# Feed-forward weights rounded and split by pieces of three tiles instead of tile by tile

## The reference

```
x = x + gate_msa * (attention(modulate(layernorm(x))) @ W_proj + b_proj)
x = x + gate_mlp * (gelu(modulate(layernorm(x)) @ w1 + b1) @ w2 + b2)
```

## Time and profile before

| | |
|---|---|
| median of 3 runs | 2257.18 us (2246.01 to 2261.7) |
| profiled execution | span 2257.0 us; no time around the span is listed for it |
| mean granted clock of TensorE | 0.932 of full speed |
| PE busy | 2033.0 us, 90% of the span |
| DVE busy | 1335.6 us, 59% |
| ACT busy | 1143.6 us, 51% |
| DMA | 173.97 MB moved, mean 77 GB/s |
| instructions | 38969 |

### The profile page before, as it was taken

One profiled execution on the slowest core, in us unless ns is written; L12 is line 12 of the kernel. 1 busy time (PEld: TensorE's weight loads), 2 busy tenths in 40 slices (PEclk: granted clock), 3 DMA queues, 4 the chain that ended last, 5 costly groups with the idle time before them and its releaser, 6 DMA issues.

```text
span 2257.0 us, 38969 instructions
## 1 busy us (share of the span) xinstructions
PE 2033.0 (90%) x15592; PEld 1509.0 (67%) x15592; DVE 1335.6 (59%) x2940; ACT 1143.6 (51%) x1705; POOL 207.4 (9%) x311
## 2 busy tenths in 40 slices
PE   6978899899989998999799899899888898999898
PEld 4347388658966994788375657788786556464658
DVE  4757637756774767476556673462444849484833
ACT  2444624574655456445626464552443464637373
POOL 2000001202100211012010000011000000000001
PEclk9787989899989999999889999998898998999999
DMA  5333332343333233333322313346254141314011
GB/s 158 77 123 57 100 95 72 79 111 86 89 77 106 72 89 76 96 94 88 94 72 35 103 17 65 73 88 109 34 95 130 7 121 26 99 11 115 9 14 25
DMA packets 204731, 173.97 MB, mean 77 GB/s; under 512 B 54822, under 2 KB 164678, under 8 KB 204550
## 3 DMA queue, kind: packets, MB, share of 16 engines
q1 hardware_dynamic: 197974, 158.76, 30.1%
q0 software_dynamic: 6576, 12.71, 2.1%
HBM read 125.57 MB, written 40.11 MB: 73 GB/s over the span
## 4 chain that ended last, share of the span: by engine, by line
PE 63%; DVE 18%; ACT 12%; DMA 3%; issue 2%; SPq 2%; POOL 0%; ACTq 0%; POOLq 0%; DVEq 0%
PE PSA L1856 16%; PE PSA L1871 13%; DVE MX L1496 7%; PE PSA L1647 5%; PE PSA L1760 5%; PE PSA L1737 5%; ACT PB L1345 4%; PE PSA L1707 4%; PE PSA L1750 4%; PE PSA L1719 2%; DVE FL L1396 2%; PE PSA L1780 1%; ACT FH L1375 1%; PE PSA L1670 1%; DVE HH L1626 1%
## 5 line engine op out<-in xcount | busy, mean ns | idle before, releaser
L1496 DVE TENSOR_REDUCE MX<-PSA 128x1 f32<-128x512 f32 x768 | 490.4, 682 | 296.9 <-PE PSA L1737 293.2
L1856 PE MATMUL PSA<-A,FH 128*128 128x256 f32 x2520 | 445.3, 292 | 12.5 <-DVE HH L1626 9.6
L1871 PE MATMUL PSA<-FH,HH 128*128 128x288 f32 x2016 | 447.7, 313 | 2.0 <-DVE HH L1626 2.0
L1382 ACT ACTIVATE HH<-PSA 128x512 fp32r<-128x512 f32 x252 | 150.4, 597 | 572.5 <-PE PSA L1856 567.3
L1345 ACT ACTIVATE PB<-PSA 128x1024 f32<-128x1024 f32 x384 | 370.9, 1025 | 102.5 <-PE PSA L1750 101.8
L1856 PEld LDWEIGHTS PSA<-A,FH 128*128 128x128 f32 x2520 | 364.9, 195 | 34.6 <-issue 17.3
L1871 PEld LDWEIGHTS PSA<-FH,HH 128*128 128x128 f32 x2016 | 329.7, 195 | 42.3 <-issue 38.0
L1871 PE MATMUL PSA<-FL,HH 128*128 128x288 f32 x1008 | 303.7, 301 | 0.0
L1737 PE MATMUL PSA<-KS,QS 54*128 54x512 f32 x768 | 226.1, 517 | 40.0 <-DVE MX L1496 14.0
L1255 POOL TENSOR_TENSOR X<-X,TM 128x288 f32<-128x288 f32 x128 | 101.1, 808 | 1496.7 <-DVE TM L1561 1496.6
L1760 PE MATMUL PSA<-PB,VT 128*32 128x512 f32 x1536 | 219.6, 637 | 0.0
(11 more groups left out here) (166 smaller groups left out, 2261.5 us busy)
## 6 DMA issues: line engine op xcount, KB each, us to landing
qkd<-HH SPq DMA_DIRECT2D x48, 504.0 KB
ST<-in_L_cond_w SPq DMA_DIRECT2D x51, 432.0 KB
ST<-in_L_cond_w SPq DMA_DIRECT2D x102, 192.0 KB
QS<-qkd SPq DMA_DIRECT2D x88, 144.0 KB
KS<-qkd SPq DMA_DIRECT2D x88, 144.0 KB
QS<-qkd SPq DMA_DIRECT2D x144, 72.0 KB
KS<-qkd SPq DMA_DIRECT2D x144, 72.0 KB
ST<-in_L_cond_w SPq DMA_DIRECT2D x153, 48.0 KB
```

Source lines behind the costliest of these rows:

```text
L1382: e.activation(r(HH[u][:, 0, :]), PS[bk][:, :], gelu)
L1496: e.reduce_max(MX[p // 2 % 2][:, col:col + 1], PS[bk][:, :], axis=AX.X).then_inc(free[bk], 1)
L1856: m = e.matmul(PS[bk][:, s_ * 256:(s_ + 1) * 256], r(w_), r(x_[:, half * 256:(half + 1) * 256]), start=(z == 0), stop=(z == 6))
L1871: m = e.matmul(PS[bk][:, 0:C], r(HH[u][:, c, tk]), r(w_), start=False, stop=(j == NCH - 1 and z == 2))
```

## The change

The three instructions per tile become three per piece. `prep_f` is called once per piece, when the `fc2` of slot 2, 5 or 8 has been put. One cast on ACT takes 128 x 2016 elements and waits for the last uses of all three slots. One subtraction on DVE corrects the tail rows of the three tiles (33 x 3 x 128, a pattern with a stride from tile to tile), one writes the low parts of the three (128 x 3 x 544). All three tiles of a piece count as ready when these are done (`w_ready` is the same count for all). The transfers, the buffers, the matmuls and every other weight stay.

```diff
@@ plan(), prep_f
-    n_f, f_at, b2_free = [0], [0], {}
+    n_f, b2_free = [0], {}
 
     def prep_f():
-        n_ = n_f[0]
-        k, x = n_ // 3, n_ % 3
+        k = n_f[0]
         if k >= len(PIECES):
             return
         n_f[0] += 1
+        n_ = 3 * k
         if n_ % NCH == 0:
             put("b2in", k, n_ // NCH)
-        if x == 0:
-            yield from arrive(("f", k))
-            f_at[0] = stage(("f", k))
-        at, m = f_at[0], n_split[0]
+        yield from arrive(("f", k))
+        at, m = stage(("f", k)), n_split[0]
         n_split[0] += 1
-        put("split", ("f", n_), at, landed[at], m, w_free.get(("F", n_ % NCH)))
+        put("split", ("f", n_), at, landed[at], m, [w_free[("F", n_ % NCH + x)] for x in range(3) if ("F", n_ % NCH + x) in w_free])
         yield
         yield
         yield
         put("fix", ("f", n_), at, m)
-        w_ready["f", n_] = m + 1
+        for x in range(3):
+            w_ready["f", n_ + x] = m + 1
+        left[at] = ("split", m + 1)
         yield
-        if x == 2:
-            left[at] = ("split", m + 1)
-            ahead()
-            yield
+        ahead()
+        yield
         if n_ % NCH == 0:
             put("b2", n_ // NCH, b2_free.get(n_ // NCH % 2))
             yield
@@ ffn_steps, fc2
-                    bg.append(prep_f())
+                    if j % 3 == 2:
+                        bg.append(prep_f())
@@ before the loop over the items
-    bg += [prep_f() for _ in range(NCH)]
+    bg += [prep_f() for _ in range(NCH // 3)]
@@ split_of
-            return (FH[:, j * NHT:(j + 1) * NHT], FL[:, j * NLT:(j + 1) * NLT], key[1] % 3 * NHT, NHT, NLT,
-                    (NLT, 128))
+            return (FH[:, j * NHT:(j + 3) * NHT], FL[:, j * NLT:(j + 3) * NLT], 0, 3 * NHT, NLT, (NLT, 128))
@@ act_program, split
-                    if old is not None and key[0] == "f":
-                        w.wait_ge(*old)
+                    if key[0] == "f":
+                        for done in old:
+                            w.wait_ge(*done)
@@ dve_program, fix
+                    if key[0] == "f":
+                        def three(t, p0, p1, f0, step, n):
+                            return view(t, p0, f0, [(1, p1 - p0, True), (step, 3, False), (1, n, False)])
+
+                        st = ST[k % 2][:, :]
+                        e.tensor_tensor(r(three(hi, 64, R2 - 1, f0, NHT, nf)), three(st, 64, R2 - 1, f0, NHT, nf),
+                                        three(hi, 64, R2 - 1, f0, NHT, nf), ALU.subtract).then_inc(s_wfix, 1)
+                        e.tensor_tensor(r(three(lo, 0, 128, 0, NLT, nl)), three(st, 0, 128, 0, NHT, nl),
+                                        three(hi, 0, 128, 0, NHT, nl), ALU.subtract).then_inc(s_wlo, 1)
+                        continue
```

## The result

The changed kernel takes 2341.35 us (median of 4 runs, 2336.54 to 2343.43) against 2259.44 us for the kernel before in the same comparison (4 runs, 2246.01 to 2262.4). The ratio is 1.0373, with a 95% interval from 1.0339 to 1.0407: it is slower by 3.7%. The forecast was 2326 us. The profiled execution has a span of 2334.8 us, 77.8 more than before, and a mean granted clock of 0.921 against 0.932.

A forecast was written before the change was run, and what follows sets the result against it. PE was taken to bound the changes of experts. Waits +60, earlier waits -8, clock +18, item ends +3 and savings -4 gave +69 us on 2257.0: 2326 us, range 2272 to 2366.

The forecast's parts named there:

- What bounds the stage: Layer 0, one expert following another: PE sets the pace, busy 33.62 of 34.00 us; idle ACT or DVE time is worth nothing.
- The prices: Grouped instructions per piece: cast 1.876 us, tail 0.556, low part 1.859; over 57 pieces ACT saves 21 us, DVE 36.
- third rival: Grouped instructions save nothing, each piece ends 0.8 us later and both stretches lose the clock: 2373 us; chance 14%.
- The waits of a change: At each change of experts fc1 waits five times for casts and low parts, 5.84 us, taken as 5.5.
- 60 - 8: Eleven changes of experts in layer 0 add 60 us of PE waits; the earlier 8.4 us of waits go.
- The clock: After PE's waits the granted clock falls, once per change of experts at 1.7 us: +18 us, between 0 and 37.
- second rival: PE waits at the changes of experts but the clock holds: 2308 us, or 2292 with more score pairs; chance 22%.
- The ends of an item and the savings: Later staging buffer and transfers at four item ends: +3 us; ACT and DVE savings elsewhere on the chain: -4 us.
- first rival: Less overhead, no slower: a piece's 4.44 us from last use to low part fit under PE's work: 2238 us; chance 14%.

The follow-up runs named there:

- e5: Changed kernel with the pieces in the eleven direct changes of experts prepared tile by tile, the other 24 still grouped by three: 2261.64 us, 1.0018 of the kernel before.
- e7: Changed kernel plus 462 overwritten filler matmuls on PE ahead of three fc1 steps in each direct change of experts: 2308.38 us, 1.0218 of the kernel before.
- e3: Changed kernel with feed-forward pieces taken as arrived after 6,000 instead of 14,000 ns of model time, so third pieces are cast earlier: 2296.94 us.
- e8: Changed kernel with groups of one and two tiles in direct changes, whole pieces elsewhere, arrival taken at 6,000 ns: 2254.04 us, 0.9981 of the kernel before.
- e6: Kernel before, tile by tile, with feed-forward pieces taken as arrived after 6,000 instead of 14,000 ns of model time: 2250.36 us, 0.9971 of before.

## Why the prediction was right, point by point

- **What bounds the stage.** Right. PE, not ACT or DVE, sets the pace of a change of experts: DVE and ACT together lost 47.5 us of work and the kernel became 82 us slower.
- **The prices.** Right to 2 ns each: 1.876, 0.556 and 1.859 us foreseen, 1.874, 0.555 and 1.859 measured. The third rival (grouped instructions save nothing) fell with them. What the casts save was too high: 21 us of ACT's busy time foreseen, 11.5 measured. The forecast had taken three times 0.75 us, but three in a row take 2.06, so that two instructions fewer save 0.19 us, 0.093 each, some 11 us over 57 pieces. Since ACT does not set the pace, this moved nothing. The Trainium skill, page "Perfetto Trace Analysis", section "Optimizing Scalar/DVE Operations", gives about 93 ns of overhead for an instruction of ScalarE on SBUF; this case's trace agrees.
- **The waits of a change.** Right in place, order and size. Foreseen 0.86, 1.33, 1.19, 0.56 and 1.90 us, 5.84 in all; measured 0.79, 1.22, 0.92, 0.54 and 1.74, 5.21. All 52 waits lie in the eleven direct changes, five in eight of them and four in the three where the first is missing, 5.4 us per change where the sum had 5.5. Over the run they grew by 51.5 us where the sum had 60 - 8 = 52. e5 shows that these eleven changes hold the loss.
- **The clock.** Right in kind, mis-sized: +18 in the sum, +29.5 us of busy time in the profile. That this is the clock can be worked out from the mean granted clocks: 0.068 of 2257.0 us were lost before and 0.079 of 2334.8 after, 153 and 184 us, an estimate of 31 us more. In the four stretches it is 23.7 us, 2.2 per change where I had taken one fall of 1.7. The rest lies outside the step that I reckoned, and part of it cannot be the change's. In the first 100 us, before any feed-forward piece is cast, the clock is lower in the profile after (the last line) than before:

```profile
0.00:100.00 100.00, 76.84 (x298) 44.34 (x298) 55.85 (x119) 28.40 (x38) 20.70 (x37) 0.80 0.44 120
0.00:100.00 100.00, 78.18 (x284) 44.54 (x286) 53.46 (x114) 26.56 (x36) 20.67 (x37) 0.74 0.46 119
```

The router's matmuls took 5.8 us more (21.8 to 27.6); those of items 1, 2 and 3 ran at a granted clock of 0.50, 0.63 and 0.50 (windows 443 to 449, 646 to 651 and 882 to 887 us), before at 0.75, 0.96 and 1.00 (430 to 436, 618 to 621 and 831 to 834.5). e7 shows that the loss goes when the pauses are filled, and e3 that it does not follow their sum; which pauses bring the clock down stays open. The second rival (the clock holds, 2308 us) is out.
- **The ends of an item and the savings.** +3 and -4 were foreseen; what the two large terms leave is 77.8 - 81.0 = -3.2. The three ends between the stretches added 0.5 us with their attention stages, and the wait for the transfer shown is the same 3.56 us.
- **The first rival (less overhead, no slower).** Its point of decision was that the 4.44 us from last use to low part fit under PE's work. They don't in the changed kernel. In e8 the smaller groups of the direct changes do fit, and the gain still isn't there: between e6 and e8 the overhead saved is 33.6 us of busy time on two engines that PE does not follow, and the time does not fall. The Trainium skill, page "Perfetto Trace Analysis", section "Optimizing Scalar/DVE Operations", says that grouping can help a saturated engine, and that breaking up may help where an unsaturated one makes others stand. The second half is borne out by e5 and the changed kernel; no engine that was grouped here was saturated, so no run shows the first. The Trainium skill, page "VectorE: DVE Perf Modes", section "The TRN2 errata", says that each instruction pays a fixed cost that a large tile pays once. The trace agrees, with 187 ns on ACT and 156 to 160 on DVE by the prediction's lines; that alone did not say what it was worth in this stage.

The 15 us between the forecast and the measured median are the clock's 11.5 us and 6.5 us by which the profiled span lies below the median time of its kernel (4.8 between executions, 1.7 around the span), less 2.7 for the other terms.

## What to carry to other kernels

Before joining small instructions into a large one, walk through one hand-over of its buffer: the large one starts at the *last* release and is done for the *first* reader only at its end. If that time doesn't fit under the bounding engine's work, the joined instruction is paid in full there for the wait, and it may be paid again for the clock behind it: here 23.7 us on top of 51.5 in the changed kernel, 0.5 on top of 33.0 in e3. Where one engine bounded the stage, fewer instructions on the others were worth nothing here; look instead at whether their work could start earlier, as e6 did by one number, for 0.3% of the time.

## What was not expected of the hardware

In the windows shown, PE's pauses of 1.22 and 0.92 us go with a granted clock of 0.70 and 0.74 in the six microseconds that begin between them; the same change of experts ran at 1.00 with the pauses filled. In the four stretches this cost nearly half as much as the waits themselves, 23.7 us beside 51.5; in e3, whose waits grew by 33.0 us, it cost 0.5, or 7.4 against e6. Matmuls that compute nothing that is used gave more back than they took: 61.0 us of them saved 46.8 of waits and 42.5 of busy time.
